# A windowed-attention block merged with a selective scan: the bf16 broadcast of B issued three times

## What is computed

```python
def step(h_prev, t):
    x_t, dt_t, B_t, C_t = t
    dA = jnp.exp(dt_t[..., None] * A)                    # 16 states per channel
    dBx = (dt_t * x_t)[..., None] * B_t[:, :, None, :]
    h = dA * h_prev + dBx
    y = jnp.einsum('bkdn,bkn->bkd', h, C_t)
    return (h, y)
```

## Time and profile before

| | us |
|---|---|
| median of 2 runs | 23726.78 |
| the two runs | 23686.44, 23767.13 |
| profiled execution, time | 23592.88 |
| its span, first to last instruction | 23590.9 |
| mean granted TensorE clock in it | 0.719 |

### The profile page before, as it was taken

One profiled execution on the slowest core, in us unless ns is written; L12 is line 12 of the kernel. 1 busy time (PEld: TensorE's weight loads), 2 busy tenths in 40 slices (PEclk: granted clock), 3 DMA queues, 4 the chain that ended last, 5 costly groups with the idle time before them and its releaser, 6 DMA issues. The chain is left out here.

```text
span 23590.9 us, 324977 instructions
## 1 busy us (share of the span) xinstructions
PE 19474.3 (83%) x96064; PEld 7726.4 (33%) x96064; DVE 19105.3 (81%) x23738; ACT 10774.5 (46%) x20618; POOL 17745.1 (75%) x14036
## 2 busy tenths in 40 slices
PE   8987888898887988989988788899988867777731
PEld 5532333333332333333333233333333211111111
DVE  5557888888876888888887688888888689999976
ACT  3344555545544445444454455544455434444420
POOL 0036888888874788888786688887788489999977
PEclk9986777666778667666678777666667876777665
DMA  0034455444545445444454545444444455555556
GB/s 18 14 130 124 96 103 103 97 95 96 103 106 168 89 98 100 95 95 92 91 102 131 145 96 100 98 96 96 90 98 97 161 128 123 119 117 120 121 134 167
DMA packets 1323235, 2508.72 MB, mean 106 GB/s; under 512 B 88168, under 2 KB 1066832, under 8 KB 1306224
## 3 DMA queue, kind: packets, MB, share of 16 engines
q1 hardware_dynamic: 1321584, 2489.33, 48.1%
HBM read 1981.62 MB, written 507.38 MB: 106 GB/s over the span
## 5 line engine op out<-in xcount | busy, mean ns | idle before, releaser
L1859 POOL TENSOR_TENSOR m_pr<-m_hs,m_c_u 128x448 f32<-128x448 f32 x8064 | 9048.1, 1136 | 2579.5 <-DVE m_hs L1742 2137.5
L1377 PE MATMUL m_psum<-m_pr,m_red 128*64 128x224 f32 x32256 | 6414.3, 501 | 221.0 <-ACT m_y_sb L1558 151.9
L1722 DVE TENSOR_TENSOR m_psum<-m_psum,m_u_u 128x448 f32<-128x448 f32 x5040 | 3094.2, 614 | 2231.0 <-PE m_psum L1367 2210.1
L1742 DVE TENSOR_TENSOR_SCAN m_hs<-m_da_t,m_carry,m_psum 128x448 f32<-128x448 f32 x4320 | 4790.2, 1128 | 37.6 <-ACT m_da_t L1572 29.6
L1841 POOL TENSOR_TENSOR m_dbp<-m_u_u,m_bp_u 128x448 f32<-128x448 f32 x3024 | 3424.7, 1133 | 112.2 <-DMA m_c_u<-scr_bc 112.2
L1367 PE MATMUL m_psum<-m_br_u,m_sel 48*128 48x448 bf16 x5040 | 2343.6, 465 | 1235.5 <-DVE m_hs L1742 1085.8
L1572 ACT ACTIVATE m_da_t<-m_dt_u,m_a_neg 128x448 f32<-128x448 f32 x5040 | 3257.7, 657 | 54.8 <-DMA m_c_u<-scr_bc 53.5
L1377 PEld LDWEIGHTS m_psum<-m_pr,m_red 128*64 128x64 f32 x32256 | 2171.1, 175 | 2802.6 <-issue 1636.3
L1742 DVE TENSOR_TENSOR_SCAN m_hs<-m_psum,m_carry,m_dbp 128x448 f32<-128x448 f32 x2592 | 2948.5, 1138 | 0.7
L1133 POOL TENSOR_TENSOR c_pr<-c_hs,c_c_u 128x784 f32<-128x784 f32 x1536 | 2803.7, 1847 | 189.6 <-DVE c_hs L1097 189.6
L1040 ACT ACTIVATE c_psum<-c_dt_u,c_a_neg 128x784 f32<-128x784 f32 x1536 | 1410.4, 918 | 2147.9 <-DVE c_hs L1097 2116.5
(11 more groups left out here) (176 smaller groups left out, 26030.8 us busy)
## 6 DMA issues: line engine op xcount, KB each, us to landing
m_c_u<-scr_bc SPq DMA_DIRECT2D x672, 896.0 KB
m_dt_u<-scr_dt SPq DMA_DIRECT2D x672, 336.0 KB
m_u_u<-scr_u SPq DMA_DIRECT2D x672, 336.0 KB
m_bp_u<-scr_bc SPq DMA_DIRECT2D x672, 336.0 KB
c_c_u<-scr_bc SPq DMA_DIRECT2D x128, 1568.0 KB, 26.8
scr_dt<-p_dt_o SPq DMA_DIRECT2D x128, 1176.0 KB, 4.5
scr_u<-p_u_o SPq DMA_DIRECT2D x128, 1176.0 KB, 5.5
c_dt_u<-scr_dt SPq DMA_DIRECT2D x128, 588.0 KB, 7.4
```

The costliest lines, as they stand in the source:

```text
L1377: mm = pe.matmul(Y[64 * h:64 * h + 64, :], red[:], pr[:, s % RP, HT * h:HT * h + HT], start=(p == 0 and opens(w)), stop=(p == NPR - 1))
L1722: nc.vector.tensor_tensor(slot(s), slot(s), u_u[:, d, s // NPR, :], ALU.mult).then_inc(mul_done, 1)
L1742: nc.vector.tensor_tensor_scan(hs[:, s % RH, way], decay(w, s)[:, way], data, init, ALU.mult, ALU.add).then_inc(scan_done, 1)
L1859: nc.gpsimd.tensor_tensor(pr[:, s % RP, :], hs[:, s % RH, :], c_u[:, d, s % NPR, :], ALU.mult).then_inc(prod_done, 1)
```

## The change

In the merged stage, `spread` issues its matmul three times with the same selection, the same moving operand and the same PSUM slot, each one starting the accumulation anew (`start=True`), so the slot holds the same values. Only the third one counts up `b_full`.

```diff
                 after(pe, scan_done, STEPS * (WI * b + w) + s - RS + 1)
-                pe.matmul(slot(s), sel[:, s % NPR, :], br_u[:, d, :], start=True, stop=True).then_inc(b_full, 1)
+                for _ in range(3):
+                    mm = pe.matmul(slot(s), sel[:, s % NPR, :], br_u[:, d, :], start=True, stop=True)
+                mm.then_inc(b_full, 1)
```

## The result

| | before, us | after, us |
|---|---|---|
| median | 23726.78 | 25858.64 |
| the runs | 23686.44, 23767.13 | 25797.45, 25919.83 |
| profiled execution | 23592.88 | 25919.83 |
| mean granted TensorE clock in it | 0.719 | 0.707 |

The change makes the kernel slower: the ratio of the times is 1.0899, with a 95% interval of 1.0762 to 1.1035. By the medians that is 2132 us.

The account below looks back on a forecast made before the run. PE was taken to end last in most of the merged stages, delaying DVE, then POOL; 22.1 us per period gave 2090 us, which with 23592.88 and the median's 134 us made 25820 us, range 24900 to 27100.

Parts of the forecast that it names:

- The stretches: Five parts of an 84-step period: 1 MLP; 2 MLP's end, q, k, v; 3 scores, softmax; 4 transposes, attention, projection; 5 second norm.
- stretches 2 and 4: End of MLP with q, k, v, and transposes with attention and projection: PE ends last; predicted growth 5.5 and 7.2 us.
- The slow repeat, 0.373 us: Merged spread: one more matmul at the slow clock costs its stream of 448 columns, 0.373 us.
- I take 0.25 us, the upper side: Merged spread: cost of one repeat at the fast clock, chosen between 0.187 and 0.27 us.
- The rest, 0.10 us, is the change of operands: From a spread to the reduction behind it: 0.10 us beyond the stream of 448 columns, at either clock.
- I take two thirds of the idle time in the mixed stretches: PE's idle time per period, 20.0 us, takes part of 35.4 us of repeats, leaving 22.1 us of growth.
- In stretch 3 the repeats are hidden by DVE's own 35.70 us: Scores and softmax: DVE ends last, so 8.2 us of repeats add only 0.9 us.
- the clock sinks: Rival: slow clock persists past the MLP into q, k, v; 26820 us if a third of periods go so; chance 0.10.
- stretch 2: End of the MLP, q, k, v: PE full at clock 1.00, all 5.5 us of repeats exposed.
- The repeats are hidden: Rival: DVE, not PE, bounds the merged stages and swallows the repeats; 23750 us, within 2%; chance 0.04.
- The repeats hold the clock up, and it gets faster: Rival: filled gaps keep PE at clock 1.00 over the whole period; 940 us saved, 22790 us; chance 0.05.
- two break-even clocks: Merged stages' mean clock needed to break even: about 0.80 by 2 us per 0.01, or 0.90 on a line.

Follow-up runs that it names:

- e8: Kernel before, with three added matmuls of 48 rows of a constant tile ahead of the spread, only at softmax and second-norm steps: 24432.51 us, ratio 1.0299.
- e6: Kernel before, with two added 448-column matmuls of 128 rows of a constant tile ahead of every merged spread: 23066.1 us, ratio 0.9715.
- e3: Kernel before, with three broadcasts only at steps 26 to 46 and 63 to 78 of each period (scores, softmax, second norm): 24569.46 us, ratio 1.0365.

## Why the prediction was right, and which of its terms were not

25820 us were predicted and 25858.64 measured, inside the range and on the predicted side. Growth by the medians is 2132 us against 2090. The agreement is better than its terms, and partly luck. The sum was for the merged stages, which should have grown by 2090 us; in the traces they grew by 2331. The total comes closer because the prediction added the 134 us by which the profiled execution of before lies under its median, while that of after lies 61 us above its own. The stretches:

| growth of a stretch, us | 1 | 2 | 3 | 4 | 5 | sum |
|---|---|---|---|---|---|---|
| predicted | 3.6 | 5.5 | 0.9 | 7.2 | 4.9 | 22.1 |
| measured, mean of 87 periods | 7.4 | 5.6 | 1.1 | 6.8 | 3.0 | 23.9 |

- **The mechanism held.** PE's stream grows, DVE waits for the spread, POOL for DVE. Its own signs came out: spread waits above 4000 us (4451.0), PE above 93% (95.6), DVE's busy time unchanged (12705 against 12656), clock inside 0.66 to 0.72 (0.68), softmax near 36 us (35.8), stretches 2 and 4 longer by 5 us or more (5.6, 6.8), stages at 17302 us against some 17050, nothing moved outside them.
- **The slow repeat, 0.373 us, was right; the fast one was not.** "I take 0.25 us, the upper side": it is 0.19. The pair of the earlier trace rows was misread as fast: the clock rose in the middle of it, and its mean clock is 0.85 (window 20003.11 to 20003.60). The next pair of the same trace that is fast throughout takes 20016.15 - 20015.71 = 0.44 us, 0.15 above the fast spread of the earlier trace rows, and 336/2.4 is 0.14: nothing besides the stream.

```profile
20003.11:20003.60 0.49, 0.49 (x5) 0.13 (x3) 0.49 (x2) 0.00 (x0) 0.40 (x1) 0.85 1.04 205
```

```profile
20015.71 0.50 PE L974 MATMUL c_psum<-c_br_u,c_sel 48*128 48x512 bf16 x2 [1.49 <-DVE c_dbx L1077]
20016.15 0.88 PE L985 MATMUL c_psum<-c_pr,c_red 128*64 128x392 f32 x4
```

The Trainium skill ("TensorE: Matmul & The Clock Gate", Back-to-back issue gap) gave an estimate of 0.19 us, and the trace agrees. The sum over the stages should have been 2900 us, not 3230 to 3350.
- **"The rest, 0.10 us, is the change of operands"** is too wide a name. In e8 the operands change from the 48-row constant to B's, and the spread starts 0.19 us behind the constant, one stream; behind the 128-row constant in e6 it starts 0.10 us later than that. It is the change between 48 and 128 rows that costs, in these pairs. The last section has the rows.
- **The idle time that takes repeats was put too high.** "I take two thirds of the idle time in the mixed stretches", 13.3 of 20.0 us per period. 8.1 us were taken. Half of the miss is the period read: it had 3.6 us idle in the MLP and 20.0 in all, the mean has 1.1 and 16.1. The two misses cancelled: the mean period got 30.2 us of repeats (2900/96) where 35.4 were put, and gave 8.1 us of idle time where 13.3 were. That leaves 22.1, the very number of the prediction. The remaining 1.8 us falls to the old work, which fits a clock that is 0.01 lower at the 2 us that the earlier trace rows give for it, but was not measured by itself.
- **"In stretch 3 the repeats are hidden by DVE's own 35.70 us"** held as far as that stretch is concerned (1.1 us). But e3 shows that the repeats of the softmax and the second norm together are not paid only where they stand: the MLP behind them grows by 3.7 us per period, with a clock that rises later. Which of the two stretches does it was not tried. The prediction looked for each repeat's cost in its own stretch, and its 3.6 us for the MLP, 7.4 measured, is the term that was furthest off.
- **The clock.** Over the period it moved by 0.01, within the 0.03 allowed. Inside, it was the MLP that lost, 0.69 to 0.62. So *the clock sinks* was right on where ("keep the slow level where it now ends in the MLP") and wrong on the price: stretch 2 stayed at 0.99.
- **The repeats are hidden** falls: 8.1 us of idle time were taken, not 16.1. **The repeats hold the clock up, and it gets faster** falls for this change and holds for its 128-row twin, e6. Of the two break-even clocks that the prediction gave, 0.80 and 0.90, the higher one is refuted: e6 is 3% faster at 0.89. A straight line through the change (180.3 us at 0.68) and e6 (151.2 us at 0.89) passes the 156.5 us of before at about 0.85, an estimate; no run lies there with the same number of added matmuls. The Trainium skill ("TensorE: Matmul & The Clock Gate", Why this matters for your kernels) asks for an engine without idle gaps. The runs here say that this alone is not enough: e8 and the change leave PE idle for 8.9 and 8.0 us per period against 16.1 before, at clocks of 0.70 and 0.68 against 0.69.

**Open:** what it is about 48 and 128 rows that the clock answers to; why the loose repeats of e3 pull the MLP's clock to 0.63 while e8's fillers, more of them and nearly in the same steps, leave it at 0.68; and why one execution of e6 ran at 0.555.

## What to carry over

- An extra matmul on an engine whose stream is in order costs its columns over the granted clock, less the idle time that it finds (here 8.1 of 30.2 us per period), and more or less what the clock then does elsewhere. Measure idle time and clock over many periods, not in one, and check by a window that a row taken for fast is fast from end to end.
- Look at the clock before the columns: an engine can be full and stay at 0.50. Three added matmuls with all 128 rows ahead of a spread, in a slot that is about to be overwritten and in steps where PE had slack, took 3.7% off this kernel; the same ones with 48 rows added 3.0%. With more of them, in the attention too, it was 5.6%. Such fillers need many executions before they are trusted: those at every spread had one execution in four at 35757 us.

## What the runs showed of the hardware

- The granted clock depends on which matmuls run, not only on how busy the engine is. For the same added columns and the same number of matmuls, the merged stages ran at 0.68 with 48-row repeats and at 0.89 with 128-row ones; with the same constant in the same places at 0.70 (48 rows) and 0.85 (128 rows).
- The number of rows does not change a matmul's own stream, but the step from 128 rows to 48 has a price. In e6 two 128-row matmuls take 0.47 us at the fast clock up to the spread behind them, 0.10 us more than two streams of 0.19 us. In e8 three 48-row ones take 2462.26 - 2461.68 = 0.58 us up to the spread, three streams and nothing more, although its operands are others:

```profile
9658.39 0.54 PE L1369 MATMUL m_psum<-m_warm 128*128 128x448 bf16 x2
9658.86 0.36 PE L1370 MATMUL m_psum<-m_br_u,m_sel 48*128 48x448 bf16 x1
```

```profile
2461.68 0.74 PE L1370 MATMUL m_psum<-m_warm 48*128 48x448 bf16 x3
2462.26 0.35 PE L1371 MATMUL m_psum<-m_br_u,m_sel 48*128 48x448 bf16 x1
```

- The load of the weights before each repeat, though of the same selection, costs nothing that can be seen: repeats stand 0.19 and 0.37 us apart, which is their stream, with 10080 more loads in PEld's count.
